# A convolution step that opens with the last step's sums and both projections of the next, on one core

## The reference, cut to what matters

```python
# GINE convolution, N = 6250, E = 100000, width 256, edges sorted by dst
msg = relu(x[src] + edge_attr @ We + be)            # E x 256
aggr = segment_sum(msg, dst, num_segments=N)
z = x + aggr                                        # on to two dense layers
# mixer over the same 6250 rows
x_mid = layernorm(fx) @ Wx.T + bx                   # pieces yT, x
k = softmax(x_mid @ Wk.T, axis=-2); v = x_mid @ Wv.T   # pieces k (the maximum), kv
kv = einsum('bhns,bhnd->bhsd', k, v)                # ctx
h = (softmax(x_mid @ Wq.T) ... kv) @ Wo.T + bo + fx # pieces q, sm, qT, mix
y = gelu(layernorm(h) @ W1.T + b1) @ W2.T + b2 + h  # pieces ln, y2T, m1, m2
```

## Time and profile before

| | us |
|---|---|
| median of 3 runs | 2700.95 (2700.74 to 2704.62) |
| profiled execution | 2702.96 |
| its span, first to last instruction | 2701.3 |
| of it, the 98 steps (about) | 110 to 1256 |
| PE busy over the span | 2030.3 (75%) |
| DVE, ACT, POOL busy | 1444.2, 759.3, 1691.1 |

### The profile page before, as it was taken

One profiled execution on the slowest core, in us unless ns is written; L12 is line 12 of the kernel. 1 busy time (PEld: TensorE's weight loads), 2 busy tenths in 40 slices (PEclk: granted clock), 3 DMA queues, 4 the chain that ended last, 5 costly groups with the idle time before them and its releaser, 6 DMA issues. The chain is left out here.

```text
span 2701.3 us, 31226 instructions
## 1 busy us (share of the span) xinstructions
PE 2030.3 (75%) x10560; PEld 1371.9 (51%) x10560; DVE 1444.2 (53%) x2751; ACT 759.3 (28%) x1268; POOL 1691.1 (63%) x1686
## 2 busy tenths in 40 slices
PE   2498997999999999998985999999999930000028
PEld 2355764556566666565663666666666620000016
DVE  7486775665666666654785334334334320006984
ACT  2243443334343344332452112112112100000015
POOL 0476774676676777663554777777777777774401
PEclk9699998999999999999996999999999975555559
DMA  7975567444444544443343222222222221113627
GB/s 214 290 204 166 170 183 264 131 138 136 135 142 137 143 141 138 118 125 108 113 121 91 53 52 57 55 50 56 57 49 57 56 33 17 17 17 110 208 75 324
DMA packets 273593, 320.76 MB, mean 119 GB/s; under 512 B 98721, under 2 KB 228214, under 8 KB 272408
## 3 DMA queue, kind: packets, MB, share of 16 engines
q0 software_dynamic: 68416, 133.35, 20.3%
q1 hardware_dynamic: 160552, 144.95, 17.6%
q10 hardware_dynamic: 44464, 40.43, 4.5%
HBM read 241.24 MB, written 77.32 MB: 118 GB/s over the span
## 5 line engine op out<-in xcount | busy, mean ns | idle before, releaser
L778 POOL DMA_INDIRECT c_xg<-xb_dram,src x784 | 786.6, 1003 | 356.3 <-issue 232.2
L2175 POOL DMA_INDIRECT er<-row_dram,gi x784 | 740.5, 945 | 240.3 <-issue 229.8
L2594 PE MATMUL ps_c<-eo,shift 128*128 128x256 f32 x294 | 68.1, 389 | 438.2 <-ACT shift L2558 434.6
L2253 PE MATMUL ps_em<-zT_all,ew 128*128 128x512 f32 (+1 forms) x832 | 351.6, 575 | 15.8 <-DMA eb_r<-in_eb 15.5
L2272 PE MATMUL ps_en<-ew,hid 128*128 128x256 f32 x1568 | 347.0, 379 | 0.6 <-DVE deg L2388 0.6
L2272 PEld LDWEIGHTS ps_en<-ew,hid 128*128 128x128 f32 x1568 | 297.5, 190 | 61.0 <-issue 23.2
L2318 ACT ACTIVATE hid<-ps_em,eb 128x512 f32<-128x512 f32 (+1 forms) x208 | 137.3, 663 | 569.0 <-PE ps_em L2253 568.6
L2413 DVE TENSOR_TENSOR eo<-ps_en,eb_r 128x1024 f32<-128x1024 f32 (+1 forms) x52 | 60.5, 1163 | 424.0 <-PE ps_en L2272 424.0
L2594 PEld LDWEIGHTS ps_c<-eo,shift 128*128 128x128 f32 x294 | 55.9, 194 | 450.2 <-issue 442.8
L805 PE MATMUL ps_e<-c_we,c_eaT 64*128 64x256 f32 x1568 | 227.6, 409 | 37.9 <-DVE c_xg L1134 33.4
L1134 DVE TENSOR_TENSOR c_xg<-ps_e,c_xg 128x1024 f32<-128x1024 f32 x196 | 235.2, 1216 | 11.2 <-DMA c_xg<-xb_dram,src 7.7
(11 more groups left out here) (299 smaller groups left out, 2700.9 us busy)
## 6 DMA issues: line engine op xcount, KB each, us to landing
c_eaT<-in_eaT SPq DMA_DIRECT2D x196, 128.0 KB
eo_dram<-eo ACTq DMA_DIRECT2D x48, 512.0 KB, 3.0
eo<-eo_dram SPq DMA_DIRECT2D x8, 2048.0 KB, 11.8
c_xg<-xb_dram,src POOLq DMA_INDIRECT x784
er<-row_dram,gi POOLq DMA_INDIRECT x784
c_xl<-xn_dram SPq DMA_DIRECT2D x24, 512.0 KB, 5.0
c_xm<-xm_dram SPq DMA_DIRECT2D x24, 512.0 KB, 4.4
erow<-c_none ACTq DMA_DIRECT2D x1, 10240.0 KB, 45.7
```

What stands on the lines that cost most here:

```text
L778: pool.indirect_dma_start(xg[:, k % NB, b, :], None, M["xb_dram"], bass.IndirectOffsetOnAxis(ap=M["src1"][:, k * B + b:k * B + b + 1], axi ...
L2175: pool.indirect_dma_start(er[:, r, b, :], None, M["row_dram"], bass.IndirectOffsetOnAxis(ap=gi[:, r, b:b + 1], axis=0)).then_inc(s_get[r], 16)
L2253: m = pe.matmul(ps_m[n % (KE - 1)][:, 0:w], w1[:, e, k, c * P:(c + 1) * P], xT[:, k, at], start=(k == 0), stop=(k == KD - 1))
```

## The change

Three loops are written in another order; no operation is added or removed. On PE a step k now opens with `add_up(k - 1)` and both halves of `project(k + 1)`, and the four groups of pieces follow with only `turn_sums(k - 1)` between the second and the third. On VectorE `add_rows(k + 1, 0)` moves from behind the third group to the head of the step, and `add_rows(k + 1, 1)` from its end to behind the first group. On ScalarE `rise` is done one step ahead, behind the first and the second group.

```diff
@@ PE
                 for k in range(S1):
+                    if k:
+                        add_up(k - 1)
                     if k + 1 < S1:
-                        project(k + 1, 0)
+                        for x in range(2):
+                            project(k + 1, x)
                     units(k, 0)
+                    units(k, 1)
                     if k:
                         turn_sums(k - 1)
-                    units(k, 1)
-                    if k + 1 < S1:
-                        project(k + 1, 1)
                     units(k, 2)
-                    add_up(k)
                     units(k, 3)
+                add_up(S1 - 1)
                 turn_sums(S1 - 1)
@@ ScalarE
+                for x in range(2):
+                    rise(0, x)
                 for k in range(S1):
                     if k:
                         save_sums(k - 1)
-                    rise(k, 0)
                     units(k, 0)
-                    rise(k, 1)
-                    for p in range(1, POINTS):
-                        units(k, p)
+                    if k + 1 < S1:
+                        rise(k + 1, 0)
+                    units(k, 1)
+                    if k + 1 < S1:
+                        rise(k + 1, 1)
+                    units(k, 2)
+                    units(k, 3)
                 save_sums(S1 - 1)
@@ VectorE
                 for k in range(S1):
+                    if k + 1 < S1:
+                        add_rows(k + 1, 0)
                     units(k, 0)
+                    if k + 1 < S1:
+                        add_rows(k + 1, 1)
                     units(k, 1)
                     if k + 1 < S1:
                         compare(k + 1)
                     units(k, 2)
                     if k:
                         add_window(k - 1)
-                    if k + 1 < S1:
-                        add_rows(k + 1, 0)
                     units(k, 3)
-                    if k + 1 < S1:
-                        add_rows(k + 1, 1)
                 add_window(S1 - 1)
```

## The result

The changed kernel takes 2768.55 us (2767.14 to 2774.5, four runs) against 2701.02 for the kernel before, run beside it: 67.5 us more, a ratio of 1.0251, 95% interval 1.0233 to 1.0269. The forecast was 2734, slower by 33: the sign and the range held, the size was half. (A ratio here takes only runs in the faster of the chip's two states, so it can differ by some tenths of a per cent from the quotient of the medians.) Of the runs behind this page, eleven (e1 to e4, f0 to f3, g0, h1, n1) fell in surroundings where every kernel, the one before too, takes about 3265 us; the reading rests on the seven others, in which the kernel before takes 2700 to 2703.

A forecast was written before the change was run, and what follows sets the result against it. The prediction took PE to bound the kernel. Its terms, −28.8 + 24 + 14 + 11 + 10 + 3 = +33 us on the median of 2700.95, gave 2734 us, with a range of 2688 to 2777.

The forecast's parts named there:

- What bounds, and the waits that go: Convolution stage: PE sets the time; projections' waits for VectorE to free their `ps_e` tile all go, 28.8 us off.
- kv pieces, steps 12 to 24: Additions and sorting delay the chain of fill, subtraction and copy behind the step's head: 24 us more, lower bound 12.
- x and k pieces, steps 1 to 11: ReLU delays reads of `x` and `yT`, addition and compare delay `k`: 1.3 us a step, 14 us more, bounds 5 and 22.
- q to m1 and `turn` in steps 27 to 97: VectorE reads `q` late before piece m1, 11 us; transposes start late behind `across`, 10 us; bounds together 8 and 35.
- Steps 25 and 26: Chains through VectorE: sums that stood inside a wait now stand ahead of it, 3 us more, bounds 0 and 6.
- The gathers: I take nothing.: Gathers have one step where they had two; 10.4 us of issue fit an average step of 11.5, so cost nothing.
- C: Rival: gathers bind; after two short steps VectorE waits at the second addition, 43 us on top, 2777; chance 0.10.
- B: Rival: losses half as large, as engines that fall behind no longer idle at the head; +2, 2703; chance 0.13.
- A: Rival: cover holds and only the projections' waits go, nothing new appears; 2672, faster; chance 0.17.
- D: Rival: new gaps lower PE's clock in steps 12 to 24, 43 us on top of the forecast, 2777; chance 0.05.
- the waits for the copy: Sign: waits of `kv` fills for ScalarE's copy grow to several times the 4.0 us.
- the new waits of m1: Sign: mixer pieces called m1 newly wait for VectorE's subtraction; no size given for this sign alone.

The follow-up runs named there:

- e1: Changed kernel with a fourth buffer of gathered rows, in the slow surroundings: ratio 1.009.
- e4: Kernel before with only the sums of a step moved to the head of the next, in the slow surroundings: ratio 1.0157.
- f0: Changed kernel, unedited, against the kernel before in the slow surroundings: ratio 0.9975.
- f3: Changed kernel with ScalarE's ReLU back in its old place, in the slow surroundings: ratio 0.9974.
- g0: Kernel before, unedited, run for its profile in the slow surroundings: ratio 0.9969.
- h1: Changed kernel with a fourth buffer of gathered rows, once more in the slow surroundings: ratio 1.0089.
- n1: Order of before up to step 26, order of m2 from step 27, four buffers of gathered rows, in the slow surroundings: 3270.2 us, ratio 1.0008.
- m1: Changed kernel with a fourth buffer of gathered rows, every engine's order kept: 2721.53 us, ratio 1.0069.
- k2: Changed kernel with the row gathers from step 3 on left out, one tiny iota per block instead: 2721.34 us, ratio 1.0077.
- k1: Kernel before with the row gathers from step 3 on left out, one tiny iota per block instead: 2698.25 us, ratio 0.9991.
- m2: Changed kernel with the sums back between pieces 2 and 3 of their own step: 2710.2 us, ratio 1.0031.
- m3: Changed kernel with ScalarE's ReLU back in its old place: 2744.18 us, ratio 1.0153.
- k4: Changed kernel with each gather from step 3 on replaced by two GpSimd iotas of set length, no transfer: 2742.84 us, ratio 1.0163.
- k3: Kernel before with each gather from step 3 on replaced by two GpSimd iotas of set length, no transfer: 2721.56 us, ratio 1.0077.

## Why the prediction was right in sign and half in size

By its own steps, net of the waits that went (the 28.8 us of the earlier trace rows lie in the four stretches as 1.9, 1.1, 0 and 25.8). "Order" is m1 less before (the gathers' room given back); "room" is the change less m1, by stretch:

| stretch | forecast | measured | order | room |
|---|---|---|---|---|
| 1 to 11 (with 1.4 to 1.6 ahead of it) | +12 | +7.7 | +7.0 | +0.7 |
| 12 to 24 | +23 | +20.0 | +20.1 | −0.1 |
| 25, 26 | +3 | +2.9 | −0.4 | +3.3 |
| 27 to 97 | −5 | +33.0 | −7.7 | +40.7 |
| sum (span) | +33 | +64 | +19 | +45 |

The pair without gathers checks the order column: k2 less k1 is +7.3, +19.3, +3.4 and −6.0 us by stretch.

- **What bounds, and the waits that go.** Right: PE sets the time, and the projections hardly wait for L1140 (over the whole span 33.4 us before, 6.5 after; in the 98 steps no such wait of PE is left).
- **kv pieces, steps 12 to 24.** Right in place, cause and size: 24 less 1.1 against 20.0, and L878 waits 27.1 us where 4.0 stood. m1, m2 and m3 all leave this wait (25.4, 18.5 and 26.3 us); with the sums in mid-step it is smallest.
- **x and k pieces, steps 1 to 11.** Somewhat too dear: 14 gross, some 9 measured with the 1.5 us ahead. 2.6 us of that difference is PE's busy time (127.6 to 125.0), the joined halves; that VectorE made up part of its delay within a step is argued, not shown.
- **q to m1 and `turn` in steps 27 to 97.** Charged 21 against 25.8 of waits gone, a net of −5; the order alone shows −7.7. The net is right by luck. From before to m1 PE's idle time rose from 46.0 to 56.7 us although the 25.8 went, so the new waits are some 36 us, just above the forecast's upper bound of 35; among them `q` waits 12.5 us for ScalarE where 2.6 stood, a place that it did not have. Against them stand 18.4 us less of busy time (770.6 to 752.2), about 15 of it the joined halves by the estimate above, where the forecast said "the work is the same as before".
- **Steps 25 and 26.** The 3 us came, but from what stays open: m1 puts them on the room (3.3, order −0.4), k2 less k1 puts 3.4 on the order, and with the sums back in mid-step (m2) the stretch is 5.7 us shorter than in m1.
- **"The gathers: I take nothing."** This is the step that failed: a term put at nothing that measured 44 to 49 us. It is more than the whole miss of 34.5 us, since the rest of the sum, +33, measured only 19 to 23. The room was reckoned right in kind (one step where two were) and wrong in size. The forecast set 10.4 us of issue against a step of 11.5, so that only the short steps mattered and "some 5 us" at the end covered them. The landing was not in it. In the timeline of the change the additions that wait for rows begin 1.9 to 5.8 us (median 2.7) after the last issue of their four gathers ended, and the second addition of a step, where it waits, 11.6 us or more (median 12.9) after the step's first issue. From the end of the sums that free the buffer to the second addition that reads it there were at least 17.7 us before (median 22.8, from step 30 on), 12.6 after (median 15.7), and at least 21.0 in m1. And it let a late gather cost VectorE alone. It stops ScalarE as well, since the early ReLU stands ahead of the mixer's reads there; with the ReLU back in its old place (m3) 24 us went, in which that share and the early ReLU's own cost are not told apart. The forecast's walks had the ReLU's 1.05 us in front of such a read, and nothing for what the ReLU itself might wait for.

**The rivals.** C was right in mechanism and place (two short steps in a row, then the second addition), and its 43 us stand beside 44 to 49. That the size fits is partly luck: C reckoned with issue time alone, and k4, which has only that, waits 5.0 us. Its chance of 0.10 was the error, since its own test, short steps followed by longer ones, was answered by a remark and not by a walk through steps 47 to 51. The total is below C's 2777 because the order alone, 2721.5 (m1), lies between B and the forecast. A is out: steps 12 to 24 grew by 20 us. D is out: in no stretch did the clock fall by itself; the 0.96 went with the stalls. The rule of the Trainium skill, page "TensorE: Matmul & The Clock Gate", section "HAM oscillation — how this bites in real kernels", that bursts between idle gaps run at half clock, is seen at single places, as in the 3.75 us of `q` at a granted clock of 0.50 after 8.30 us of idle, and in m1 in its 3.19 us at 0.60 after 2.52; over steps 12 to 24 the clock stayed at 1.00 with 27.1 us of idle time.

Of the signs it named, the waits for the copy, the new waits of m1, VectorE idle at the head (207.7 us before L1140, 69 times where about a hundred were named) and the gathers' 60.2 us came; steps 12 to 24 missed 155 by 0.4; steps 1 to 11 took 146.7 where about 154 was named; "steps 27 to 97 within 10 us of 816.6" is the one that broke.

## What to carry to other kernels

When a reader of a transfer is moved forward, sum the whole time of that transfer, issue, landing and the backlog of the queue behind a run of short steps, and set it against the new distance from the event that frees its buffer to the read; a mean step length hides exactly the steps that bind. Then look at each in-order queue that the late reader stands in: everything behind it is late too, and so is whatever waits for it on the next engine. One more buffer gives such a loss back with no change of order (47 us here), and is the cheapest experiment to tell it from the cost of the order itself. And price an instruction group anew when its neighbours change: two halves of a projection, 0.2 us cheaper joined than apart, made a term as large over the steps as the waits that were forecast.

## What the runs showed of the hardware that was not expected

**Work on GpSimd slows one kind of VectorE instruction.** The groups of one line of VectorE in k1, then in k3, where GpSimd runs iotas of 0.56 us most of the time; then the additions and one line of the sort, each in k1 and in k3:

```profile
L1254 DVE TENSOR_SCALAR xn<-c_h,c_mv,c_rs 128x256 f32<-128x256 f32 x49 | 16.9, 408 | 0.0
...
L1254 DVE TENSOR_SCALAR xn<-c_h,c_mv,c_rs 128x256 f32<-128x256 f32 x49 | 29.4, 658 | 0.0
...
L1144 DVE TENSOR_TENSOR c_xg<-ps_e,c_xg 128x1024 f32<-128x1024 f32 x194 | 232.7, 1216 | 3.5 <-PE ps_e L812 2.6 <-POOL c_idle L782 0.3 <-issue 0.3
...
L1144 DVE TENSOR_TENSOR c_xg<-ps_e,c_xg 128x1024 f32<-128x1024 f32 x194 | 232.6, 1215 | 3.0 <-PE ps_e L812 2.1 <-issue 0.5 <-POOL c_idle L782 0.2
...
L1705 DVE TENSOR_TENSOR c_key<-c_key 128x512 f32<-128x512 f32 x125 | 85.7, 685 | 0.0
...
L1705 DVE TENSOR_TENSOR c_key<-c_key 128x512 f32<-128x512 f32 x125 | 85.7, 686 | 0.0
```

TENSOR_SCALAR goes from 408 to 658 ns, TENSOR_TENSOR stays at 1216, and with both inputs in SBUF (L1705, a sort stage) at 685. The gathers themselves do not do this: in the kernel before, where they keep GpSimd busy, the same TENSOR_SCALAR takes 411 ns. VectorE is busy for 542.65 us instead of 520.38 in steps 27 to 97, and the stretch takes 834.3 us instead of 814.1. That this is the 23 us between k1 and k3 is argued, not shown. The Trainium skill, page "SBUF — State Buffer", section "SBUF: two separate sides", says that VectorE in a two-port mode and GpSimd take turns on one pair of ports, each for a whole instruction, and that a VectorE instruction with two SBUF inputs meets this only where GpSimd reads SBUF; the iotas read nothing, and the 685 and 686 ns agree. That TENSOR_SCALAR at 408 ns runs in a two-port mode is shown by no run here, so for the 658 ns the rule is a possible cause and no more.

**The same program at 2700 and at 3265 us.** From 1779 to 1871 us, in the edge stage behind the convolution, the changed kernel in its first trace and in f0 (columns as in the stretches above):

```profile
1779.00:1871.00 92.00, 92.00 (x431) 62.46 (x431) 33.46 (x24) 17.48 (x26) 69.58 (x74) 1.00 0.28 52
...
1779.00:1871.00 92.00, 48.96 (x207) 30.92 (x205) 16.14 (x11) 7.73 (x12) 54.32 (x59) 0.76 0.21 36
```

Half the matmuls in the same time, 207 where 431 were. In f0 VectorE ends an addition at 1791.1, ScalarE issues a transfer at the same time, and both compute again only from 1822.8 on, which the timeline puts down to DMAs long past:

```profile
1822.75 0.23 DVE L2394 TENSOR_TENSOR deg<-ps_en,deg 128x64 f32<-128x64 f32 x1 [31.64 <-DMA g_om<-om_dram]
```

The gathers take as long in both (1001 ns beside 1004). The time lies in standstills, in the two stages in which GpSimd issues 784 gathers each; ahead of the first gather, in the stage between the two and in the last stage, which has 49 gathers of its own, the two traces keep the same pace (the lag of f0 stays at 138.4 us from 1363 to 1503). It is no property of one chip: m1 and h1, the same kernel on the same chip, took 2721.53 and 3308.18 us. What causes the standstills is open. For an experiment it means: run the unedited kernels beside the edits, and where they do not show the difference that is to be explained, their neighbours can't explain it.
